# Causal attention: the transfers that fill the stacked operands move from SyncE's queue to ScalarE's, and the first keys' transposes move to another PSUM bank

## The reference

```python
q = jnp.einsum('bsm,hmd->bshd', resid, W_Q) + b_Q
k = jnp.einsum('bsm,hmd->bshd', resid, W_K) + b_K
v = jnp.einsum('bsm,hmd->bshd', resid, W_V) + b_V
q = _apply_rotary(q, sin, cos, ROT_DIM)
k = _apply_rotary(k, sin, cos, ROT_DIM)
k = jnp.concatenate([k, virtual_k], axis=1)      # 16 more keys, v likewise
scores = jnp.einsum('bqhd,bkhd->bhqk', q, k) / SCALE
mask = jnp.arange(kv_len)[None, :] <= jnp.arange(s)[:, None] + VKV
pattern = softmax(where(mask, scores, -inf))
z = jnp.einsum('bhqk,bkhr->bqhr', pattern, v_g)
out = jnp.einsum('bqhd,hdm->bqm', z, W_O)
```

## Time and profile before

| | us |
|---|---|
| median of 3 runs | 1700.04 |
| lowest, highest | 1693.35, 1711.82 |
| the profiled execution, by the same clock | 1705.34 |
| its span in the profile | 1703.5 |
| attention stage of the change, about | 40 to 645 |

### The profile page before, as it was taken

The page is one execution under the profiler, slowest core; times in us unless marked ns, Lnnn a source line. Parts: engine busy times, 40 slices in busy tenths (PEclk is TensorE's granted clock), DMA queues, the critical chain, the costliest instruction groups (busy, mean ns, idle before and its releaser), DMA issues. The chain is left out here.

```text
span 1703.5 us, 34646 instructions
## 1 busy us (share of the span) xinstructions
PE 1486.0 (87%) x11556; PEld 940.7 (55%) x11556; DVE 1221.7 (72%) x3703; ACT 1121.9 (66%) x2657; POOL 440.8 (26%) x442
## 2 busy tenths in 40 slices
PE   4689998989989884688888888769999999999996
PEld 2255555556556552366666666645555555555564
DVE  4377777777777765688878888762577877877755
ACT  1267676776767762467777767626688788787852
POOL 0333333333333314454444444320000000000001
PEclk9599999999999997799999999985699999999998
DMA  1577777778777745111001110008899999999930
GB/s 40 155 191 193 189 184 195 185 194 199 188 180 189 186 106 185 26 26 31 20 19 31 27 25 22 11 11 254 228 320 309 298 316 319 299 316 305 305 102 25
DMA packets 154896, 272.84 MB, mean 160 GB/s; under 512 B 27920, under 2 KB 31200, under 8 KB 154592
## 3 DMA queue, kind: packets, MB, share of 16 engines
q1 hardware_dynamic: 154720, 270.63, 56.4%
HBM read 148.03 MB, written 112.98 MB: 153 GB/s over the span
## 5 line engine op out<-in xcount | busy, mean ns | idle before, releaser
L519 ACT ACTIVATE a_Pm<-a_Pm,a_nm 128x272 f32<-128x272 f32 (+3 forms) x512 | 266.7, 570 | 165.9 <-DVE a_nm L441 165.6
L441 DVE CUSTOM_DVE_ANT_0 a_Pm<-ps,a_mask 128x272 f32<-128x272 f32 (+3 forms) x512 | 237.7, 503 | 90.8 <-PE ps L358 89.3
L1899 DVE CUSTOM_DVE_ANT_0 r_Sx<-ps,r_Sx 128x512 f32<-128x512 f32 x256 | 166.7, 689 | 136.1 <-PE ps L1634 135.7
L1773 ACT COPY r_BD<-ps 128x320 f32<-128x320 f32 x512 | 193.6, 429 | 101.6 <-PE ps L1621 88.4
L1634 PE MATMUL ps<-r_K,r_qu 32*128 32x256 f32 x1024 | 233.9, 453 | 0.6 <-DVE r_nb L1899 0.6
L1621 PE MATMUL ps<-r_R,r_qv 32*128 32x320 f32 x1024 | 230.5, 521 | 1.9 <-ACT r_BD L1773 1.1
L358 PE MATMUL ps<-a_Kst,a_Qst 128*128 128x272 f32 (+4 forms) x640 | 203.3, 414 | 13.4 <-DMA a_Kst<-bounce 13.2
L358 PEld LDWEIGHTS ps<-a_Kst,a_Qst 128*128 128x128 f32 x640 | 114.6, 195 | 143.5 <-issue 64.5
L1780 ACT ACTIVATE r_Sx<-r_Sx,r_nb 128x512 f32<-128x512 f32 x256 | 187.9, 734 | 5.1 <-DVE r_nb L1899 5.0
L1644 PE MATMUL ps<-m_ident,r_Sx 128*128 128x128 f32 x1024 | 173.3, 295 | 0.1
L1644 PEld LDWEIGHTS ps<-m_ident,r_Sx 128*128 128x128 f32 x1024 | 113.5, 146 | 107.3 <-issue 67.7
(11 more groups left out here) (204 smaller groups left out, 2708.4 us busy)
## 6 DMA issues: line engine op xcount, KB each, us to landing
spill<-r_BD SPq DMA_DIRECT2D x256, 288.0 KB, 4.8
r_Sx<-spill SPq DMA_DIRECT2D x128, 512.0 KB, 5.6
a_Kst<-bounce SPq DMA_DIRECT2D x128, 264.0 KB, 4.9
a_Qst<-bounce SPq DMA_DIRECT2D x128, 256.0 KB, 4.4
bounce<-a_kh SPq DMA_DIRECT2D x32, 264.0 KB, 3.5
bounce<-a_kl SPq DMA_DIRECT2D x32, 264.0 KB, 4.0
bounce<-a_qh SPq DMA_DIRECT2D x32, 256.0 KB, 5.6
bounce<-a_ql SPq DMA_DIRECT2D x32, 256.0 KB, 5.9
```

Of the source, the lines that this page charges most:

```text
L441: nc.vector.tensor_tensor_reduce(out=Pm[:, u % 2, qt, 0:w], in0=S[:, S_of[qt]:S_of[qt] + w], in1=mask[:, N + AV - w:N + AV], scale=-SCALE, ...
L519: nc.scalar.activation(row, row, ACT.Exp, scale=-1.0, bias=nm[:, u % 2, qt:qt + 1]).then_inc(exp_done, 1)
L1773: nc.scalar.copy(BD[:, m % BUFS, j, HW * half:HW * half + HW], ps[:, BDB[k % 3], 0:HW]).then_inc(bd_ev, 1)
L1899: nc.vector.tensor_tensor_reduce(out=row, in0=ps[:, AC + n % 2, :], in1=row, scale=-SCALE, scalar=-BIG, op0=ALU.add, op1=ALU.min, accum_ou ...
```

## The change

SyncE only sends the halves to memory (`to_memory`) and stores outputs. The four transfers that fill the stack are issued by ScalarE: for the first step after all four splits, then at even k from 4 on, three units after the split of the same piece. `bounced` becomes one semaphore a piece. The first keys' transposes use bank TB+1 and wait for VectorE's copy of it; the wait for P0T's copy moves to TB+1's next transposes.

```diff
+    bounced = s.sems(*(f"bounced{m}" for m in range(4)))
...
-            def stack(st, m):
+            def to_memory(st, m):
                 i, k = m // 2, 4 * st + m
                 width_ = (N, KN)[m % 2]
-                dst, halves = ((Qst, (qh, ql)), (Kst, (kh, kl)))[m % 2]
+                halves = ((qh, ql), (kh, kl))[m % 2]
                 for j, (src, made) in enumerate(zip(halves, (hi_done, lo_done))):
                     sp.wait_ge(made, k + 1)
-                    sp.dma_start(bounce[st % 2][m][j, :, 0:width_], src[:, i].bitcast(F32)).then_inc(bounced, 16)
-                sp.wait_ge(bounced, 32 * (k + 1))
-                if st >= 2:
-                    sp.wait_ge(s_ready, 2 * (U * (st - 2) + GH * (i + 1)))
-                for block, j in enumerate(((0, 1, 0, 1), (0, 0, 1, 1))[m % 2]):
-                    sp.dma_start(dst[st % 2][32 * block:32 * block + 32, :, i].bitcast(F32),
-                                 bounce[st % 2][m][j, :, 0:width_].rearrange("(h c) n -> c h n", h=GH)).then_inc(stk[st % 2][i], 16)
+                    sp.dma_start(bounce[st % 2][m][j, :, 0:width_], src[:, i].bitcast(F32)).then_inc(bounced[m], 16)
...
             for m in range(4):
-                stack(0, m)
+                to_memory(0, m)
...
                     if st + 1 < STEPS:
-                        stack(st + 1, m)
+                        to_memory(st + 1, m)
...
-                    pool.wait_ge(bounced, 32 * (k - 3))
+                    pool.wait_ge(bounced[m], 32 * st)
...
                     pe.wait_ge(exp_done, 4 * u + 4)
                     if u >= 1:
                         pe.wait_ge(evd, u)
+                    if u >= GH and u % GH == 1:
+                        pe.wait_ge(p0_ev, u // GH)
                 elif u >= 1:
                     pe.wait_ge(eva, 2 * u - (1 if k == 2 else 0))
-                if k == 0 and u >= GH and u % GH == 1:
-                    pe.wait_ge(p0_ev, u // GH)
...
-                pe.wait_ge(eva, 2 * min(GH * (bb + 1) + 1, UNITS))
+                pe.wait_ge(evd, min(GH * (bb + 1) + 1, UNITS))
                 for qt in range(NT):
-                    ins = nc.tensor.transpose(ps[:, TB, P * qt:P * qt + P], P0[:, bb % 2, qt, :], c["ident"][:])
+                    ins = nc.tensor.transpose(ps[:, TB + 1, P * qt:P * qt + P], P0[:, bb % 2, qt, :], c["ident"][:])
...
-                nc.vector.tensor_copy(P0T[:], ps[:, TB, :]).then_inc(p0_ev, 1)
+                nc.vector.tensor_copy(P0T[:], ps[:, TB + 1, :]).then_inc(p0_ev, 1)
...
-                    act.wait_ge(bounced, 32 * (k - 3))
+                    act.wait_ge(bounced[m], 32 * st)
...
+            def stack(st, m):
+                i, k = m // 2, 4 * st + m
+                width_ = (N, KN)[m % 2]
+                dst = (Qst, Kst)[m % 2]
+                act.wait_ge(bounced[m], 32 * (st + 1))
+                if st >= 2:
+                    act.wait_ge(s_ready, 2 * (U * (st - 2) + GH * (i + 1)))
+                for block, j in enumerate(((0, 1, 0, 1), (0, 0, 1, 1))[m % 2]):
+                    act.dma_start(dst[st % 2][32 * block:32 * block + 32, :, i].bitcast(F32),
+                                  bounce[st % 2][m][j, :, 0:width_].rearrange("(h c) n -> c h n", h=GH)).then_inc(stk[st % 2][i], 16)
+
             for m in range(4):
                 split_hi(0, m)
+            for m in range(4):
+                stack(0, m)
             for k in range(UNITS + 1):
                 if k < UNITS:
                     exps(k)
...
                 if k % 2 == 1 and k < UNITS and k // U + 1 < STEPS:
                     split_hi(k // U + 1, k % U // 2)
+                if k % 2 == 0 and k >= 4 and (k - 4) // U + 1 < STEPS:
+                    stack((k - 4) // U + 1, (k - 4) % U // 2)
```

More of the change, by code:

```diff
@@ L220, in attention_groups @@
     names = (w0, w1, pj_ready, stt_done, added, hi_done, lo_done, s_ready, nm_ready, exp_done, t_done, evd, eva, pv_done,
-             tab_in, pad_done, ones_done, p0_done, p0_tr, p0_ev, vm_done, z_ready, z_ev, z0, z1, bounced) = s.sems(
+             tab_in, pad_done, ones_done, p0_done, p0_tr, p0_ev, vm_done, z_ready, z_ev, z0, z1) = s.sems(
         *("w0 w1 pj_ready stt_done added hi_done lo_done s_ready nm_ready exp_done t_done evd eva pv_done "
-          "tab_in pad_done ones_done p0_done p0_tr p0_ev vm_done z_ready z_ev z0 z1 bounced").split())
+          "tab_in pad_done ones_done p0_done p0_tr p0_ev vm_done z_ready z_ev z0 z1").split())
     w_in, z_out = (w0, w1), (z0, z1)
+    bounced = s.sems(*(f"bounced{m}" for m in range(4)))
     bounce = [[nc.dram_tensor(f"bounce{k}{m}", (2, P, KN), F32, kind="Internal").ap() for m in range(4)] for k in range(2)]
@@ L537, in _ @@
                     split_hi(k // U + 1, k % U // 2)
-    clear(nc, [*names, *stk[0], *stk[1]])
+                if k % 2 == 0 and k >= 4 and (k - 4) // U + 1 < STEPS:
+                    stack((k - 4) // U + 1, (k - 4) % U // 2)
+    clear(nc, [*names, *bounced, *stk[0], *stk[1]])
 def rope_tables():
```

## The result

The changed kernel takes 1760.24 us (median of 4, 1752.65 to 1766.41), the kernel before in the same session 1705.28 (median of 4, 1693.35 to 1711.82). The ratio is 1.0329, 95% interval 1.0275 to 1.0382: slower by 3.3%. The profiled execution took 1757.41 us (span 1755.6) against 1705.34, so 52 us more.

A forecast was written before the change was run, and what follows sets the result against it. TensorE was taken to set the pace in causal attention, with the just-in-time K stack as second limit. Standstill 31, clock 60 and beginning 7 made +98 us on the 1700.04 median: 1798, range 1732 to 1856.

The forecast's parts named there:

- rival B: At the attention's heads K is late as forecast, but TensorE's clock holds: 1738 us, chance 0.20.
- rival C: ScalarE issues transfers only when the copies ahead are done, K 1.85 us later: 1850 us, chance 0.13.
- the likeliest case: K stack late and clock lowered at the heads: 1798 us, own range 1775 to 1820, chance 0.51.
- The clock's term: Standstill of 2.8 us lowers TensorE's clock in a head's first two units: 2.4 us in 25 of 28 batches, +60 us.
- the standstill: TensorE waits 2.8 us a batch for the K stack, where it stood 1.5: +1.1 us, 28 times, +31 us.
- the beginning: First step's stacks issued only after ScalarE's last split: first head +9.8 us, second head's 2.58 us wait gone, net +7 us.
- The bank's gain: First keys' transposes no longer wait for ScalarE's copy: 1.47 us a batch, up to 43 us.
- The sequencer: ScalarE's sequencer stays with exponentials whose maxima are missing; first K transfer goes 0.25 us after the long exponentials start.
- Rival A: ScalarE's sequencer passes waiting exponentials, so the K stack is in time: 1664 us, chance 0.10.
- The K chain: Long exponentials at head + 11.24, K issued at + 11.5, landed at + 18.5, next head at + 18.65 us.
- The Q stack: Issued in a head's own unit and needed at the next head, 16 us on: hidden.
- The signs named ahead: Trace signs in the stage: Kst wait some 30 times 2.8 us, 80 to 90 in all; PEclk 0.8 or less; first head near 84.

The follow-up runs named there:

- bank_only: The kernel before with only the first keys' bank edit, SyncE still filling the stacks: 1702.47 us, ratio 1.0010 to the kernel before.
- sooner_old_bank: sooner_start with the first keys' transposes back in bank TB: 1697.33 us, ratio 0.9993 to the kernel before.
- between: The changed kernel with each stack issued between the short and long exponentials of its unit: 1680.65 us, ratio 0.9867 to the kernel before.
- unit_sooner: The changed kernel with each stack issued one unit sooner in ScalarE's program: 1669.05 us, ratio 0.9793 to the kernel before.
- fill_less: The changed kernel with three unused 128x512 products on TensorE ahead of each head's stack wait, from unit 8 on: 1734.48 us, ratio 1.0233.
- sooner_start: unit_sooner with the first step's stacks issued one by one, each behind the next split: 1654.63 us, ratio 0.9747 to the kernel before.
- two_sooner: sooner_start with each stack issued another unit sooner, one unit after the split: 1718.21 us, ratio 1.0121 to the kernel before.

## Why the prediction was right, and which terms were off

**The outcome.** Slower, as forecast with 0.83, and inside the range of 1732 to 1856. That range is wide enough to hold rival B (1738) and rival C (1850) too, so lying in it does not tell them apart; the likeliest case's own range, 1775 to 1820, was missed. What held is the late K stack and what holds it back; the forecast of 1798 was too high by 38 us. The clock's term was 39 us too large, the standstill's 6 and the beginning's 1; against that the kernel before came out 5 us above the 1700.04 from which the forecast starts, and 3 us lie between profiles and medians.

**The bank's gain** is there and hidden, as said: no wait of the first transposes for ScalarE in the kernel after; bank_only and sooner_old_bank show both sides of it.

**The sequencer.** "I take the first K transfer 0.25 us after the long exponentials start": measured 0.22 or 0.23 in 25 of 28 batches. This was the step on which the sign hung, and it came from the records of lines 525 and 506. More exactly, it is the missing maxima that hold the sequencer, not the start: between shows a transfer issued 0.7 us ahead of exponentials that have their maxima. Rival A, in which the stack passes waiting exponentials, would be 1664; unit_sooner, in which the program and not the queue brings the issue to 8.1 us after the head on average, is 1669. So A's arithmetic was right and its mechanism was not. Rival C, the issue behind the copies, is excluded by 166.93 against the copies after it. The Trainium skill (Perfetto Trace Analysis, "DVE / Act Engine Instruction") lets an instruction stand in a wait queue while the sequencer goes on; the traces of this case show no such pass by a transfer behind an exponential whose maxima are missing, in any run.

**The K chain.** I had the exponentials at head + 11.24 and the landing 7.0 later; at full clock they are at 10.78 and 7.39, two errors of about 0.4 us that cancel, which is luck: 18.46 from head to head where 18.65 was forecast. Of the first, 0.3 come from the head at which it was read, whose first two units took 7.34 us (301.60 to 308.94), where 174.43 to 181.48 takes 7.05. The term: 25 us instead of 31.

**The clock** is the step that failed: "I take it for 25 of 28 batches: +60 us", at 2.4 us each. The clock fell in 17 batches and cost 1.23 in each, 21 us. Both factors were read from two heads behind which the clock stayed at the lower level for the whole 6.5 us (0.51, 0.50); here it is 0.74 over such a stretch, so about half of it, and only the first unit pays. The two heads of before were also not of the repeating kind: one is the second head of the stage, one the last, with 0.72 and 1.78 in their first rows. The count fell outside the 20 to 28 batches allowed for it. Rival B, no price at all, would have been 1738 against 1760 measured; fill_less, the kernel after with the clock held, is at 1734.48. Truth lay between the forecast and B, nearer to B.

**The Q stack** hidden, **the end** unchanged: both held. **The beginning**: the first head was forecast at 84.0 and is at 83.47; +6 us in place of +7. sooner_start shows that the order of the first splits and stacks is the cause: 75.58.

**The signs named ahead.** The wait of line 353 was forecast as 30 times 2.8, 80 to 90 us; it is 31 times and 89.8, which looks like a hit but holds the first one's 14.8; the other 30 have 74.9, 2.5 each. Wrong was that the slices of the page would show 0.8 or less: the page's row of the granted clock is, after,

```profile
PEclk9599999999999998689999999986599999999998
```

and has no digit under 9 between the stage's first slices and its end: a third of a batch at 0.74, in 17 of 28 batches, makes a mean of 0.95. What the clock did is seen only in windows cut at the heads.

## What to carry to other kernels

A transfer that an engine issues between its computing instructions starts when the sequencer gets there, and here that is when the compute instruction ahead has what it waits for, not when the data are ready. So place it in the program behind the last instruction whose wait is over by then, and about where its own data are in memory; one unit too late cost 5% here, one unit too early 4%.

When two waits on one path are nearly equal, take both or neither: each half of this change alone was worth nothing or cost time, with the stack issued in time the two were worth 2.5%, 43 us. And a price that is read at one exceptional place (the first or the last turn of a loop) should be taken with a wide range.

## What the runs showed of the hardware that I had not expected

- How long TensorE had stood did not decide whether its clock fell. In the kernel after it fell behind 17 of 28 gaps of 2.03 to 3.15 us, among them 2.24 us (head 230.46, 0.74), and not behind the longest, 3.15 us (head 403.58, 1.00); gaps of 2.24 to 3.07 us brought it down and gaps of 2.03 to 3.15 did not. In bank_only it fell even behind gaps of 1.85 us (0.74 from 230.5 to 237.0) and 1.80 us (0.74 from 584.5 to 591.0) and held behind 2.07 us (1.00 from 282.8 to 289.3). The Trainium skill (TensorE: Matmul & The Clock Gate, "HAM oscillation") speaks of longer gaps; these runs show it from 1.80 us on. What decides whether a given gap lowers the clock stays open.
- When the clock falls so, it is back by the first microsecond of the second unit: behind the head of 154.71 it is 0.53 from 156.0 to 159.6 and 1.00 from there to 162.0, behind that of 192.84 it is 0.60 from 193.0 to 197.3 and 1.00 behind that. The first unit lasts 3.80 to 4.39 us then, against 2.73 to 2.75, and 1.23 us are lost by the third. Behind the two heads of the earlier trace rows it was low for over 6 us.
- A wait in ScalarE's program for a transfer that has not landed holds back the exponentials behind it even when their maxima are ready: 2.96 us in two_sooner.
- ScalarE's sequencer does not pass an exponential whose maxima are missing, and does pass one that only waits for the engine: in between the transfer goes out 0.10 us after the maxima and 0.7 us before the exponential starts.
- Four issues by ScalarE took 1.8 us, as SyncE's did, and cost ScalarE nothing that shows as long as exponentials and copies were queued ahead of them; in two_sooner, with nothing queued, they cost their whole length.
